# Attention 1: exponentials and values in one float32 product, and another order of its transfers

## The reference

```python
def _L1_xattn_ref(q, k, v, Wc, bc):
    N_HEADS, N_GROUPS, HEADS_PER_GROUP = 16, 4, 4
    HEAD_DIM = 32
    b, s, _ = q.shape
    qh = q.reshape(b, s, N_GROUPS, HEADS_PER_GROUP, HEAD_DIM).transpose(0, 2, 3, 1, 4)
    kh = k.reshape(b, s, N_GROUPS, HEAD_DIM).transpose(0, 2, 1, 3)
    vh = v.reshape(b, s, N_GROUPS, HEAD_DIM).transpose(0, 2, 1, 3)
    scores = jnp.einsum('bghsd,bgtd->bghst', qh, kh) * (1.0 / math.sqrt(HEAD_DIM))
    probs = jax.nn.softmax(scores, axis=-1)
    out = jnp.einsum('bghst,bgtd->bghsd', probs, vh)
    out = out.transpose(0, 3, 1, 2, 4).reshape(b, s, D_MODEL)
    return out @ Wc.T + bc

# x: 4 x 512 x 512, ctx_512: 4 x 512 x 128
x = x + jnp.tanh(g_xattn[0]) * _L0_xattn_ref(_layernorm(x), ctx_512, ...)
x = x + jnp.tanh(g_ffn[0]) * _L0_ffn_ref(_layernorm(x), ...)      # 8 experts, 2 of them for each token
x = x + jnp.tanh(g_xattn[1]) * _L1_xattn_ref(_layernorm(x), ctx_512, ctx_512, Wc, bc)
x = x + jnp.tanh(g_ffn[1]) * _L1_ffn_ref(_layernorm(x), ...)      # 16 experts, 6 of them for each token
return x
```

## Time and profile before

| | us |
|---|---|
| median of 3 runs | 2380.8 (2374.16 to 2385.57) |
| the profiled execution | 2375.09 |
| its span in the profile | 2373.3 |
| attention 1, first exponential to last product with the values | 787.4 to 1243.4 |

### The profile page before, as it was taken

One profiled execution on the slowest core, in us unless ns is written; L12 is line 12 of the kernel. 1 busy time (PEld: TensorE's weight loads), 2 busy tenths in 40 slices (PEclk: granted clock), 3 DMA queues, 4 the chain that ended last, 5 costly groups with the idle time before them and its releaser, 6 DMA issues. The chain is left out here.

```text
span 2373.3 us, 37291 instructions
## 1 busy us (share of the span) xinstructions
PE 1954.4 (82%) x10825; PEld 1586.0 (67%) x10825; DVE 1251.8 (53%) x2653; ACT 816.5 (34%) x1315; POOL 1017.1 (43%) x795
## 2 busy tenths in 40 slices
PE   4548879988882767887777897999999969999995
PEld 2237767766661444555554675789999969989995
DVE  6874554332223876888875666544444424434442
ACT  3451111123332565565664111123333323323331
POOL 5534633734444677566780010023433323333331
PEclk8879999999996677888888898999999989999998
DMA  9575655788966565232543000184649997574444
GB/s 340 173 243 192 189 187 197 242 299 200 268 123 142 124 188 150 35 47 34 151 154 126 27 3 27 48 316 81 158 78 280 285 306 212 122 189 78 80 82 107
DMA packets 131465, 372.74 MB, mean 157 GB/s; under 512 B 20456, under 2 KB 24424, under 8 KB 126104
## 3 DMA queue, kind: packets, MB, share of 16 engines
q1 hardware_dynamic: 81208, 265.14, 35.2%
q0 software_dynamic: 33600, 79.73, 17.8%
q10 hardware_dynamic: 16480, 25.63, 3.1%
HBM read 209.93 MB, written 151.86 MB: 152 GB/s over the span
## 5 line engine op out<-in xcount | busy, mean ns | idle before, releaser
L1599 PE MATMUL ps<-f_wb,f_xThi 128*128 x2088 | 534.8, 338 | 36.6 <-issue 28.0
L1721 POOL DMA_INDIRECT y_scratch<-f_yo,f_rows x150 | 238.3, 1589 | 487.7 <-issue 286.1
L1599 PEld LDWEIGHTS ps<-f_wb,f_xThi 128*128 128x128 f32 x2088 | 369.4, 191 | 64.8 <-issue 55.9
L1599 PE MATMUL ps<-f_wb,f_xTlo 128*128 x1044 | 345.7, 331 | 0.0
L1618 PE MATMUL ps<-f_wb,f_hThi 128*128 (+2 forms) x822 | 276.6, 418 | 23.2 <-DVE f_hTlo L1952 22.6
L724 POOL TENSOR_TENSOR a_elo<-a_e,a_ehi 128x768 f16<-128x768 f32 x128 | 216.6, 1697 | 135.3 <-ACT a_ehi L792 134.0
L1970 DVE TENSOR_TENSOR f_g<-ps,f_bb 128x352 f32<-128x352 f32 x111 | 58.2, 525 | 339.5 <-PE ps L1599 333.9
L1694 POOL DMA_INDIRECT f_xg<-xn_scratch,f_rows x150 | 159.7, 1065 | 169.5 <-PE ps L1583 118.9
L1599 PEld LDWEIGHTS ps<-f_wb,f_xTlo 128*128 128x128 f32 x1044 | 199.3, 191 | 0.0
L971 DVE TENSOR_REDUCE a_nmax<-ps 128x1 f32<-128x512 f32 x256 | 164.0, 681 | 48.2 <-PE ps L826 47.8
L1444 ACT ACTIVATE f_yo<-ps,f_share 128x512 f32<-128x512 f32 x150 | 103.4, 689 | 245.6 <-PE ps L1618 219.6
(11 more groups left out here) (247 smaller groups left out, 3952.6 us busy)
## 6 DMA issues: line engine op xcount, KB each, us to landing
f_wb<-w_scratch SPq DMA_DIRECT2D x16, 2816.0 KB
w_scratch<-f_stage_up SPq DMA_DIRECT2D x27, 1024.0 KB
w_scratch<-a_stage_up SPq DMA_DIRECT2D x25, 1024.0 KB, 5.4
f_stage_raw<-in_f_w_dram SPq DMA_DIRECT2D x29, 768.0 KB, 7.1
f_wb<-w_scratch SPq DMA_DIRECT2D x16, 1024.0 KB
w_scratch<-f_stage_down SPq DMA_DIRECT2D x108, 128.0 KB
w_scratch<-a_stage_down SPq DMA_DIRECT2D x100, 128.0 KB, 2.4
f_wb<-w_scratch SPq DMA_DIRECT2D x8, 1536.0 KB, 9.4
```

Source lines behind the costliest of these rows:

```text
L1599: mm = pe.matmul(out, xt[:, b % 2, k, :], weights(at, w, k, low), start=(m == 0), stop=(m == 3 * KD - 1))
L1721: pool.indirect_dma_start(y_d, bass.IndirectOffsetOnAxis(ap=rows_of[:, b:b + 1], axis=0), yo[:, b % 3, :], None, bounds_check=ROWS + SPARE ...
```

## The change

Two things at once, in attention 1 alone.

1. The exponential is taken once, stays float32 and is the stationary operand as it is; values stay float32, 32 columns and one of ones. The parts `ehi`, `elo` and their subtractions, the three parts of the values, the sum over them (L987), and the semaphores between go away. The scaling reads PSUM itself, so the next head's first product now waits for the scaling (`o_ready`) and not for the sum.
2. Transfers: in a static unit the store of the last chunk (`put`) stands ahead of the strips, and the loads (`ask`) stand apart from the stores and come before the row maxima and the unit's first store. The row maxima's DMAs move from ScalarE to SyncE. The casts of a chunk come a step later (`UPPER`, `LOWER`).

```diff
@@ tiles and constants of cross_attention_1 @@
-    VC = 3 * HD + 1
+    VC = HD + 1
-    CUT = 256
-        vres = sb(ctx, "a1_vres", [P, NT, DC])
-        v3 = sb(ctx, "a1_v3", [P, NT, GROUPS, VC + 1], BF16)
+        vrest = sb(ctx, "a1_vrest", [P, 1024])
+        v1 = sb(ctx, "a1_v1", [P, NT, GROUPS, VC])
-        ehi = sb(ctx, "a1_ehi", [P, 4, 2, S], F16)
-        elo = sb(ctx, "a1_elo", [P, 4, 2, S], F16)
-        osum = sb(ctx, "a1_osum", [P, TB, HD])
-        def split_step(u, j, lag):
-
-            n, w = divmod(j - lag, 4)
-            i = chunk_of(u, n) if w < 3 else None
-            return (i, (w,)) if i is not None else (0, ())
+        UPPER = {1: (0, (0,)), 2: (0, (1,)), 3: (0, (2,)), 5: (1, (0,)), 6: (1, (1,)), 7: (1, (2,))}
+        LOWER = {2: (0, (0,)), 3: (0, (1,)), 4: (0, (2,)), 6: (1, (0,)), 7: (1, (1, 2))}
...
@@ SyncE @@
+                maxima(0, 0)
                 sp.wait_ge(v_ready, 1)
...
-                def keep(u, n):
+                def put(u, n):
                     i = chunk_of(u, n)
                     if i is not None:
                         stage.store(sp, i, *later(i))
-                        if i + 2 < LATER:
-                            stage.load(sp, i + 2, *later(i + 2))
+
+                def ask(u, n):
+                    i = chunk_of(u, n)
+                    if i is not None and 2 <= i + 2 < LATER:
+                        stage.load(sp, i + 2, *later(i + 2))
 
                 def unit(u, grp, has_prepare, has_maxima, wc_batch):
+                    static = isinstance(u, int)
+                    if static and grp > 0:
+                        put(u - 1, 1)
                     if has_prepare:
                         strips(u + 2, (grp + 2) % GROUPS)
-                        if not (isinstance(u, int) and u + 3 == UNITS):
+                        if not (static and u + 3 == UNITS):
                             load(u + 3, (grp + 3) % GROUPS)
-                    if isinstance(u, int):
-                        if grp > 0:
-                            keep(u - 1, 1)
-                        keep(u, 0)
+                    if static and grp > 0:
+                        ask(u - 1, 1)
+                    if static:
+                        ask(u, 0)
+                    if has_maxima:
+                        maxima(u + 1, (grp + 1) % GROUPS)
+                    if static:
+                        put(u, 0)
                         if grp == GROUPS - 1:
-                            keep(u, 1)
+                            put(u, 1)
+                            ask(u, 1)
@@ GpSimd @@
-                pool.wait_ge(vhi_ready, 1)
-                pool.tensor_tensor(v_res, v_raw, v_hi, ALU.subtract).then_inc(vres_ready, 1)
                 prepare_pool(pool, 2, 2, 0)
-                pool.wait_ge(vmid_ready, 1)
-                pool.tensor_tensor(v_lo, v_res, v_mid, ALU.subtract).then_inc(v_ready, 1)
...
                         pool.wait_ge(exp_done, n + 1)
-                        e, h, l = (m.rearrange("p i s -> p (i s)")[:, CUT:] for m in
-                                   (e32[:, j % 4, :, :], ehi[:, j % 4, :, :], elo[:, j % 4, :, :]))
-                        pool.tensor_tensor(l, e, h, ALU.subtract).then_inc(lo_pool, 1)
...
@@ ScalarE @@
-                act.copy(v_hi, v_raw).then_inc(vhi_ready, 1)
                 prepare_scalar(act, 1, 1)
+                act.copy(v1[:, :, :, 0:HD], vraw[:].rearrange("p t (g d) -> p t g d", g=GROUPS)).then_inc(v_ready, 1)
...
-                        wait(act, lo_dve, n - 3)
-                        wait(act, lo_pool, n - 3)
+                        wait(act, pv_done, n - 3)
                         act.wait_ge(sc_ready, n + 1)
                         act.activation(e32[:, j % 4, :, :], ps[:, 2 * (j % 2):2 * (j % 2) + 2, :],
-                                       ACT.Exp)
-
-                        wait(act, pv_done, n - 3)
-                        act.activation(ehi[:, j % 4, :, :], ps[:, 2 * (j % 2):2 * (j % 2) + 2, :],
                                        ACT.Exp).then_inc(exp_done, 1)
-                        stage.high(act, act.copy, *split_step(u, j, 0))
+                        stage.high(act, act.copy, *split_step(u, j, UPPER))
-                        if j == 6 and has_maxima:
-                            maxima_rows(act, u + 1, (grp + 1) % GROUPS)
@@ TensorE, pv_tensor @@
-                    wait(pe, sum_ready, 4 * u + j // 2)
-                pe.wait_ge(lo_dve, n + 1)
-                pe.wait_ge(lo_pool, n + 1)
+                    wait(pe, o_ready, 4 * u + j // 2)
+                pe.wait_ge(exp_done, n + 1)
                 for t in range(TB):
                     for i in range(2):
-                        for part in (ehi, elo):
-
-                            mm = pe.matmul(ps[:, PV_BANK, P * t:P * t + VC], part[:, j % 4, i, P * t:P * t + P],
-                                           v3[:, bass.ds(TB * b + 2 * (j % 2) + i, 1), grp, 0:VC],
+
+                        mm = pe.matmul(ps[:, PV_BANK, P * t:P * t + VC], e32[:, j % 4, i, P * t:P * t + P],
+                                       v1[:, bass.ds(TB * b + 2 * (j % 2) + i, 1), grp, 0:VC],
...
@@ VectorE @@
-            def sum_vector(dve, u, grp, q):
+            def head_vector(dve, u, grp, q):
...
-                dve.reciprocal(rden[:], out[:, :, 3 * HD]).then_inc(rden_ready, 1)
-                dve.tensor_reduce(osum[:], out[:, :, 0:3 * HD].rearrange("p t (c d) -> p t d c", c=3), AX.X,
-                                  ALU.add).then_inc(sum_ready, 1)
-
-            def head_vector(dve, u, grp, q):
-                h = HPG * u + q
+                dve.reciprocal(rden[:], out[:, :, HD]).then_inc(rden_ready, 1)
                 dve.wait_ge(rden_ready, h + 1)
-                dve.wait_ge(sum_ready, h + 1)
                 at = P * grp + HD * q
-                dve.tensor_tensor(otok[:, :, at:at + HD], osum[:], rden[:].unsqueeze(2).to_broadcast([P, TB, HD]),
-                                  ALU.mult).then_inc(o_ready, 1)
+                dve.tensor_tensor(otok[:, :, at:at + HD], out[:, :, 0:HD],
+                                  rden[:].unsqueeze(2).to_broadcast([P, TB, HD]), ALU.mult).then_inc(o_ready, 1)
...
-                def split(u, j):
-
-                    e, h, l = (m.rearrange("p i s -> p (i s)")[:, 0:CUT] for m in
-                               (e32[:, j % 4, :, :], ehi[:, j % 4, :, :], elo[:, j % 4, :, :]))
-                    dve.wait_ge(exp_done, 8 * u + j + 1)
-                    dve.tensor_tensor(l, e, h, ALU.subtract).then_inc(lo_dve, 1)
```

More of the change, by code:

```diff
@@ L601, in later, with split_step @@
             return g["PREPARED"][g["LAST"] + i]
-        def split_step(u, j, lag):
-            n, w = divmod(j - lag, 4)
-            i = chunk_of(u, n) if w < 3 else None
-            return (i, (w,)) if i is not None else (0, ())
+        UPPER = {1: (0, (0,)), 2: (0, (1,)), 3: (0, (2,)), 5: (1, (0,)), 6: (1, (1,)), 7: (1, (2,))}
+        LOWER = {2: (0, (0,)), 3: (0, (1,)), 4: (0, (2,)), 6: (1, (0,)), 7: (1, (1, 2))}
+        def split_step(u, j, when):
+            n, pieces = when.get(j, (0, ()))
+            i = chunk_of(u, n)
+            return (i, pieces) if i is not None else (0, ())
         with nc.Block() as block:
@@ L631, in strips, with maxima @@
                                  flt(qlo[:, grp % 2, :])).then_inc(strips_in[grp % 2], 16)
+                def maxima(u, grp):
+                    sp.wait_ge(mlo_ready, u + 1)
+                    for i, m in enumerate((mhi, mlo)):
+                        sp.dma_start(flt(qs[3 * HD + i:3 * HD + i + 1, HPG * grp:HPG * grp + HPG, :]),
+                                     flt(m[:, grp % 2, :])).then_inc(m_in[grp % 2], 16)
                 load(0, 0)
@@ L728, in unit @@
                         if j == 1 and has_prepare:
-                            pool.wait_ge(lo_pool, n + 1)
+                            pool.wait_ge(xc_ready, u + 3)
+                            if isinstance(u, int) and grp > 0:
+                                pool.wait_ge(stage.lo_done, chunk_of(u - 1, 1) + 1)
+                            elif not isinstance(u, int) or u > 0:
+                                pool.wait_ge(stage.lo_done, LATER // 2)
                             keys_pool(pool, u + 2, (grp + 2) % GROUPS)
-                        stage.low(pool, *split_step(u, j, 1))
+                        stage.low(pool, *split_step(u, j, LOWER))
                 batches(pool, unit)
@@ L847, in pv_tensor @@
                 if j % 2 == 0:
[L849 to L851 removed]
+                    wait(pe, o_ready, 4 * u + j // 2)
+                pe.wait_ge(exp_done, n + 1)
                 for t in range(TB):
                     for i in range(2):
[L854 to L859 removed]
+                        mm = pe.matmul(ps[:, PV_BANK, P * t:P * t + VC], e32[:, j % 4, i, P * t:P * t + P],
+                                       v1[:, bass.ds(TB * b + 2 * (j % 2) + i, 1), grp, 0:VC],
```

(12 more changed lines are left out.)

25 lines of the change are left out of this document (6 added, 19 removed).

## The result

The changed kernel takes 2529.0 us (median of 4 runs, 2509.0 to 2540.4). The kernel before, on the same chip, takes 2380.9 (2374.2 to 2385.6). The ratio is 1.061, 95% interval 1.054 to 1.068: 6% slower. The forecast was 2440 with a range to 2515, so the sign was right, the size far off, and the time lies outside the range. The profiled execution took 2521.0 us with a span of 2519.2.

The account below looks back on a forecast made before the run. No engine was full in attention 1 (457 us); everybody waited for everybody. TensorE work of 408 us at a clock of 0.84 is 486, plus 30 us of waits 516, +59, hence 2440 us; range 2350 to 2515, the forecast's own 2393 to 2515.

Parts of the forecast that it names:

- The step that failed: TensorE's granted clock in attention 1 was taken to stay at 0.84, with bounds 0.73 and 1.0.
- TensorE's full-clock work: TensorE's own work in attention 1 at full clock was to rise from 272 to 408 us.
- The product's price: Attention 1's float32 product: 16 load and matmul pairs a step at 0.11 us, +136 us; step 2.77 us.
- rival C: Four loads for each float32 product in attention 1: 769 us for the stage, 2693 us in all; chance 0.03.
- The waits: Attention 1's waits were to fall from 133 to 30 us, left to transfers, with bounds 10 and 50.
- The new wait: In attention 1 the next head's first product waits for the scaling: taken as hidden, 0 us, bounds 0 to 19.
- VectorE's and ScalarE's savings: Attention 1: ScalarE loses 131 us, VectorE 116 and 34; worth nothing by themselves beyond ending waits that longer steps would cover.
- Rival A: The clock holds in attention 1, as TensorE hardly pauses: stage 436 us at 0.97, 2360 us in all; chance 0.21.
- Rival B: The clock in attention 1 is mostly low, 0.6: stage 695 us, 2619 us in all; chance 0.10.
- Rival D: Gain and cost cancel in attention 1, at a clock near 0.95: 2369 to 2393 us in all; chance 0.13.
- The order of transfers: In attention 1 it was to remove most of ScalarE's 38.6 us wait for chunk loads, within the 30 us left.
- All other stages keep their length: Every stage but attention 1 was to take as long as before.

Follow-up runs that it names:

- e3: The changed kernel with 97 instead of 33 moving columns in the product, the added 64 being unused ones: 2350.0 us, ratio 0.985 to the kernel before.
- e1: The kernel before with only the new order of transfers and the later casts, old product kept: 2356.7 us, ratio 0.989 to the kernel before.
- e2: The changed kernel with the old order of transfers, so the float32 product alone: 2504.2 us, ratio 1.049 to the kernel before.
- e7: The changed kernel with 97 columns in the product and the old order of transfers: 2351.9 us, ratio 0.989 to the kernel before.
- e5: The changed kernel with 65 instead of 33 moving columns, the added 32 being unused ones: 2383.9 us, ratio 0.997 to the kernel before.
- e8: The changed kernel with float16 exponentials, bfloat16 values and one product of 97 columns per pair, low parts left out: 2267.6 us, ratio 0.953 to the kernel before.
- e10: The changed kernel with float16 exponentials and bfloat16 values, low parts left out, 33 columns: 2265.9 us, ratio 0.953 to the kernel before.

## Why the prediction was wrong, point by point

**The step that failed** is the last term before the sum: "I take the 0.84 of the stage as it is, with 0.73 (its worst unit) and 1.0 as bounds." It measured 0.65, below the lower bound. The sum shows its weight. TensorE's full-clock work was forecast at 408 us. Divided as the prediction divides, it is 595 x 0.65 = 387; e3, whose steps are as long at full clock, has 412 busy us at 0.97, which is 400. At 0.84 that is 461 or 476, and with the waits that remained (some 3 us) the stage would have been 464 or 479 us, 7 or 22 more than before. At 0.65 it is 595. So 116 to 131 of the 138 us are the clock, and a kernel that had kept its clock would have been less than 1% slower than the one before. The text had named what would do it, that "no stretch of this trace shows how the clock takes them", and then closed the bound with a unit of the old work. An operation that no row shows has no measured bound for its clock either: the lower end had to be the other level itself, 0.5, at which nine of the ten units with little or nothing of the projection stood for most or all of their time.

**The product's price** was right: 0.11 us for a pair (0.112), two loads for each product (2048), a step of 2.77 (2.70). The bound of 0.14 for load and product one after the other wasn't needed. By the Trainium skill (FP8 and Floating Point Precision, section TensorE Precision Notes) true float32 takes four passes. The trace again has two loads for each product, 2048 for 1024, so rival C fell.

**The waits** were too high, 30 us against 3. The predicted direction holds: `ehi`, sum and maxima no longer hold TensorE up, and the chunk's 38.6 us are gone. The new wait, taken at 0, is 0.6 us. VectorE's and ScalarE's savings bought nothing, as said; ScalarE now waits 295 us for the scores.

**Rival A** is refuted, and the reading of a rule with it. By the Trainium skill (TensorE: Matmul & The Clock Gate, section What's actually happening) activity releases the throttle, from which A took that an engine that hardly pauses keeps its clock. Busy 43.3 of 43.3 us it was granted 0.50: the profile's busy share doesn't tell the clock. e3, which has the same loads at the same pace and only more columns, is at 0.97, and its 428 us are A's 436.

**Rival B**, a mean clock of 0.6 and 695 us, had the right picture (low through whole units) but no cause for it, and was given 0.10. It had the clock fall first and stay low; here it also falls while TensorE is busy. The argument against it, that the projection comes in every batch but the first, holds for those units only: they are the ones at 0.75 to 1.00.

**Rival D** didn't come. **The order of transfers** was credited within the waits, rightly for the kernel before (24 us, e1) and wrongly for the new one, where e2 and e7 show nothing. I had not asked what the order was worth once TensorE sets the pace.

**All other stages keep their length**: nearly. From the last product to the end it is 1137 us, 1129 before; e1 has 1129 and every kernel with a single product 1134 to 1139. Some 5 us of it are two waits for gathered rows that the kernel before doesn't have:

```profile
PE ps L1552 <- DMA f_xg<-xn_scratch,f_rows: 5.0, 2, 4.3
```

Why these rows come later wasn't tried and stays open.

## What to carry to other kernels

Price an edit on TensorE at both clock levels, and ask for every stretch how much of its busy time streams columns: here float32 loads with 33 columns behind each kept the engine full and its clock mostly at half. If such a product can't be avoided, try to stream more columns through each load, useful ones or not, as long as the streaming is shorter than the load: here 64 columns of ones gave back 179 us. Then set the result against the old product with everything else that the edit brought: e3 leads the kernel before by 31 us, and e1, which has only the other order, by 7. A busy share near 100% says that the engine sets the pace, not that it runs at its speed.

Before crediting an earlier transfer, look whether the engine that sets the pace waits for it: the same order gave 24 us where it did and nothing where it didn't.

## What the runs showed of the hardware

- Granted clock 0.50 over 43.3 us in which TensorE was busy for all of them (33 columns for each float32 load), 0.97 over a stage with 97 behind the same loads.
- After a pause of 2.9 us the clock was at 0.50 for 30.8 us with 65 columns (e5); after one of 2.6 us for 3.4 us with 97 (e3). With 33 it fell after 34.1 us with 0.12 us of pauses.
- Distance of two plain float32 load and matmul pairs at full clock 0.112 us with 33, 97 and 113 columns, at half clock 0.213; of two 16-bit pairs 0.026 us with 33 and 0.044 with 97.
- Shortest distance of two float32 loads of 128x128 0.108 us, of two 16-bit ones 0.015 (e8, e10).
- VectorE's scaling 0.290 to 0.292 us once it reads PSUM and GpSimd no longer splits exponentials; with both inputs in SBUF its spread was 0.27 to 1.76 (before).
